# Which instruction carries a semaphore wait: a relation-aware graph attention layer, every repeated wait moved onto the instruction behind it

## The reference

```python
Q = (jnp.einsum('nc,rch->rnh', x, Wq) + bq[:, None, :]).reshape(R, N, HEADS, OUT)
K = (jnp.einsum('nc,rch->rnh', x, Wk) + bk[:, None, :]).reshape(R, N, HEADS, OUT)
V = (jnp.einsum('nc,rch->rnh', x, Wv) + bv[:, None, :]).reshape(R, N, HEADS, OUT)
q_i = Q[edge_type, dst]
k_j = K[edge_type, src]
v_j = V[edge_type, src]
score = jnp.sum(q_i * k_j, axis=-1) * scale
seg = dst * R + edge_type
m = jax.ops.segment_max(score, seg, num_segments=N * R)
e = jnp.exp(score - m[seg])
s = jax.ops.segment_sum(e, seg, num_segments=N * R)
alpha = e / s[seg]
out = jax.ops.segment_sum(v_j * alpha[..., None], dst, num_segments=N)
x = _layernorm(x + out.reshape(N, HD) + bias)
```

## Time and profile before

| | |
|---|---|
| median of 3 runs | 2276.77 us (2274.12 to 2283.94) |
| the profiled execution: its time / span of its instructions | 2263.78 us / 2262.0 us |
| instruction records | 33,259 |
| PE busy | 1719.4 us, 76% of the span |
| DVE busy | 1569.7 us, 69% |
| POOL busy | 1176.7 us, 52% |
| ACT busy | 1074.7 us, 48% |
| DMA | 571.56 MB, mean 253 GB/s |
| chain that ended last | PE 53%, DVE 18%, "issue" 16% |

### The profile page before, as it was taken

One profiled execution on the slowest core, in us unless ns is written; L12 is line 12 of the kernel. 1 busy time (PEld: TensorE's weight loads), 2 busy tenths in 40 slices (PEclk: granted clock), 3 DMA queues, 4 the chain that ended last, 5 costly groups with the idle time before them and its releaser, 6 DMA issues.

```text
span 2262.0 us, 33259 instructions
## 1 busy us (share of the span) xinstructions
PE 1719.4 (76%) x7549; PEld 1186.0 (52%) x7549; DVE 1569.7 (69%) x3858; ACT 1074.7 (48%) x4050; POOL 1176.7 (52%) x1254
## 2 busy tenths in 40 slices
PE   8999995227999995477777777777777777677788
PEld 4555542002444442356666566665666666566667
DVE  8888983002434442587788888887888888888877
ACT  3333320001000000066777777777777777777775
POOL 3111117773666304556666666666666666666504
PEclk9999997657999997699899999999999999999998
DMA  8998737775999747888888889888888998888733
GB/s 225 275 246 226 217 119 231 229 222 185 313 338 329 260 159 234 265 275 265 268 279 282 281 283 283 279 288 281 277 281 286 279 285 284 276 272 278 235 99 114
DMA packets 344898, 571.56 MB, mean 253 GB/s; under 512 B 44993, under 2 KB 238433, under 8 KB 344702
## 3 DMA queue, kind: packets, MB, share of 16 engines
q0 software_dynamic: 87360, 274.23, 40.8%
q1 hardware_dynamic: 224330, 234.48, 31.7%
q10 hardware_dynamic: 33012, 60.73, 7.5%
HBM read 408.84 MB, written 140.96 MB: 243 GB/s over the span
## 4 chain that ended last, share of the span: by engine, by line
PE 53%; DVE 18%; issue 16%; another core or an unknown queue 8%; ACT 3%; POOL 1%; DVEq 1%; DMA 1%; SPq 0%; ACTq 0%; POOLq 0%
PE sums L727 20%; PE sums L796 15%; PE pairs L807 12%; DVE region L1122 3%; DVE region L1323 3%; DVE region L1380 2%; PE bank L762 2%; PE bank L755 1%; DVE region L1332 1%; PE sums L854 1%; POOL region L555 1%; PE sums L865 1%; DVE region L1333 1%; DVE region L1389 1%
## 5 line engine op out<-in xcount | busy, mean ns | idle before, releaser
L555 POOL DMA_INDIRECT region<-kv_tab,kvidx x824 | 806.0, 978 | 566.5 <-issue 198.2
L727 PE MATMUL sums<-region,acc 128*128 128x512 f32 (+2 forms) x1568 | 677.8, 584 | 6.5 <-ACT acc L879 4.1
L994 ACT ACTIVATE region<-region 128x64 f32<-128x64 f32 x2368 | 655.5, 346 | 0.9
L796 PE MATMUL sums<-region 128*128 128x150 f32 x3296 | 500.4, 306 | 129.9 <-issue 125.1
L807 PE MATMUL pairs<-region 128*128 128x256 f32 x1648 | 426.1, 403 | 186.1 <-DVE region L1323 103.4
L796 PEld LDWEIGHTS sums<-region 128*128 128x128 f32 x3296 | 461.4, 199 | 188.6 <-issue 175.6
L727 PEld LDWEIGHTS sums<-region,acc 128*128 128x128 f32 (+1 forms) x1568 | 297.6, 195 | 306.7 <-issue 286.7
L807 PEld LDWEIGHTS pairs<-region 128*128 128x128 f32 x1648 | 312.5, 199 | 249.6 <-issue 210.1
L1291 DVE TENSOR_TENSOR region<-sums,region 128x512 f32<-128x512 f32 (+1 forms) x215 | 147.4, 691 | 368.2 <-PE sums L727 146.2
L1012 ACT COPY acc<-sums 128x294 f32 x824 | 327.2, 397 | 73.5 <-PE sums L796 47.4
L537 POOL DMA_INDIRECT region<-q_tab,region x288 | 274.8, 954 | 147.7 <-issue 81.0
(11 more groups left out here) (244 smaller groups left out, 967.6 us busy)
## 6 DMA issues: line engine op xcount, KB each, us to landing
region<-q_seg SPq DMA_DIRECT2D x824, 128.0 KB
kv_tab<-region ACTq DMA_DIRECT2D x42, 1280.0 KB
q_seg<-region SPq DMA_DIRECT2D x288, 128.0 KB
q_tab<-region SPq DMA_DIRECT2D x48, 640.0 KB, 4.3
region<-rel_tab SPq DMA_DIRECT2D x206, 128.0 KB
region<-region POOLq DMA_DIRECT2D x47, 384.0 KB, 5.5
region<-kv_tab,kvidx POOLq DMA_INDIRECT x824
region<-in_x SPq DMA_DIRECT2D x96, 128.0 KB, 2.8
```

The lines of the kernel that those rows point to most:

```text
L555: pool.indirect_dma_start(ring_row[:, a:a + 2 * C], None, kv_tab, bass.IndirectOffsetOnAxis(ap=kvidx[:, t:t + 1], axis=0)).then_inc(s_got[ ...
L727: done = nc.tensor.matmul(bank[o % 4][0:n, 0:w], acc[:, k, t * P:t * P + n], w_sb[:, k, :, :].rearrange("p u c -> p (u c)")[:, c0:c0 + w], ...
L796: done = nc.tensor.matmul(bank[i][:, h * W:(h + 1) * W], ring_v[:, i, spot(q), h * P:(h + 1) * P], oneh[:, q % 2, i, :], start=True, stop= ...
L994: done = nc.scalar.activation(ring_v[:, i, spot(q), h * D:(h + 1) * D], ring_v[:, i, spot(q), h * D:(h + 1) * D], ACT.Copy, scale=alT[:, h ...
```

## The change

It moves waits from `wait_ge` in front of an instruction onto the instruction itself (`wait_op`), always the last of the waits in front. No wait is dropped and no work moves. The core of the diff:

```diff
@@ -368,11 +368,12 @@
+        def evicted(o):
+
+            return (s_evA, o + 1) if o < OA else (s_evD, o - OA + 1)
+
         def wait_evicted(eng, o):
-            if o < OA:
-                eng.wait_ge(s_evA, o + 1)
-            else:
-                eng.wait_ge(s_evD, o - OA + 1)
+            eng.wait_ge(*evicted(o))
@@ -544,17 +545,17 @@
                     pool.wait_ge(s_agg, SB * (s - KS + KL + 1))
-                if s >= KL:
-
-                    pool.wait_ge(s_mul, s - KL + 1)
...
-                    pool.indirect_dma_start(ring_row[:, a:a + 2 * C], None, kv_tab,
-                                            bass.IndirectOffsetOnAxis(ap=kvidx[:, t:t + 1], axis=0)
-                                            ).then_inc(s_got[s % KL], 16)
+                    rows_in = pool.indirect_dma_start(ring_row[:, a:a + 2 * C], None, kv_tab,
+                                                      bass.IndirectOffsetOnAxis(ap=kvidx[:, t:t + 1], axis=0)
+                                                      ).then_inc(s_got[s % KL], 16)
+                    if i == 0 and s >= KL:
+
+                        rows_in.wait_op(s_mul, s - KL + 1, "sem-ge")
@@ -721,12 +723,12 @@
-                if o >= 4:
-                    wait_evicted(pe, o - 4)
                 for k in range(KC):
...
+                    if k == 0 and o >= 4:
+                        done.wait_op(*evicted(o - 4), "sem-ge")
@@ -785,9 +787,6 @@
-                    if q > 0:
-
-                        pe.wait_ge(s_cols, columns_taken(q - 1, i))
...
+                        if h == 0 and q > 0:
+
+                            done.wait_op(s_cols, columns_taken(q - 1, i), "sem-ge")
                     done.then_inc(s_agg, 1)
 
             def lift(s):
 
                 pe.wait_ge(s_gotq[s % QS], 16 * SB * (s // QS + 1))
                 pe.wait_ge(s_oht, s + 1)
-                if s > 0:
-                    pe.wait_ge(s_mul, s)
                 for i in range(SB):
                     done = nc.tensor.matmul(qk[:, i, :], oht[:, s % 2, i * P:(i + 1) * P], qring[:, s % QS, i, :],
                                             start=True, stop=True)
+                    if i == 0 and s > 0:
+                        done.wait_op(s_mul, s, "sem-ge")
@@ -1006,11 +1007,11 @@
             def place_window(q, i, at):
                 t = q * SB + i
-                act.wait_ge(s_agg, t + 1)
                 if t > 0:
                     act.wait_ge(s_placed, t)
                 nc.scalar.copy(acc[:, :, bass.ds(at[(q % 2) * SB + i] + 1, PW)],
-                               bank[i][:, 0:2 * W].rearrange("p (h n) -> p h n", h=2)[:, :, 0:PW]).then_inc(s_placed, 1)
+                               bank[i][:, 0:2 * W].rearrange("p (h n) -> p h n", h=2)[:, :, 0:PW]
+                               ).then_inc(s_placed, 1).wait_op(s_agg, t + 1, "sem-ge")
@@ -1308,25 +1309,24 @@
                 dve.wait_ge(s_got[s % KL], gathered(s))
-                dve.wait_ge(s_lift, s + 1)
                 if s > 0:
                     dve.wait_ge(s_sc, s)
-                nc.vector.tensor_tensor(prod[:], ring_k[:, :, spot(s), :], qk[:], ALU.mult).then_inc(s_mul, 1)
+                nc.vector.tensor_tensor(prod[:], ring_k[:, :, spot(s), :], qk[:], ALU.mult
+                                        ).then_inc(s_mul, 1).wait_op(s_lift, s + 1, "sem-ge")
@@ -1406,10 +1406,10 @@
                 if i == 0 or q >= SINGLE:
                     dve.wait_ge(s_cols, columns_taken(q, i))
+                added = nc.vector.tensor_tensor(acc[:, :, bass.ds(col, 1)], acc[:, :, bass.ds(col, 1)],
+                                                cols[:, q % CS, i, :, 2:3], ALU.add).then_inc(s_acc, 1)
                 if t > 0:
-                    dve.wait_ge(s_acc, t)
-                nc.vector.tensor_tensor(acc[:, :, bass.ds(col, 1)], acc[:, :, bass.ds(col, 1)],
-                                        cols[:, q % CS, i, :, 2:3], ALU.add).then_inc(s_acc, 1)
+                    added.wait_op(s_acc, t, "sem-ge")
```

## The result

The changed kernel took 2371.44 us, median of 4 executions (2365.69 to 2380.02), the kernel before 2277.84 us. The ratio is 1.041, 95% interval 1.039 to 1.043. Forecast was 2273 us, range 2253 to 2287. In a later comparison, on chip 3, it was 2340.59 against 2264.76 us, ratio 1.034 (1.031 to 1.037).

What follows compares the result with a forecast made beforehand. The loop was taken to run at the pace of POOL's gather bursts with their gap. Savings of 1.1 and 2.8 us less POOL's 0.7 made 3.2, rounded to 3.5: 2276.8 - 3.5 = 2273 us, range 2253 to 2287.

Steps and rivals of the forecast that it cites:

- the POOL exchange: Loop gathers: s_agg moves to the separate wait, losing at most 0.06 us where truly late, 0.7 us in all.
- The 12: Loop: number of steps whose gather comes just behind its aggregate, 0.27 us later, and so truly waits for it.
- The 0.06 us: Loop gathers on POOL: most that each truly late wait loses by standing in the separate instruction, priced as on PE.
- Rival B: Loop, each step's first gather: late s_agg in the separate wait costs 0.06 us, 11.3 us over 188 steps; 2285; chance 0.10.
- The other parts: Loop and its end: ACT and PE give back 1.1 us in 12 steps, the last 14 steps 2.8 us.
- rival C: Loop: a 0.1 us shift moves single steps between prompt and late news of PE's work; 2267 or 2287; chance 0.13.
- rival A: Loop: hand-offs, not POOL, set the pace; 0.20 us less in each of 206 steps, 41 us, 2236, or 2263; chance 0.22.
- The 0.09 us of the sum: Loop on ACT: saved per place_window copy whose aggregate ends last; 0.063 us from wait and arithmetic, more from earlier issue.
- The second stage: From 560 to 880 us: PE is full, so exchanged waits of evictions and chunks give 0; query gathers are not waited for.
- `lift` comes sooner: Loop on PE: lift starts 0.05 us behind products instead of 0.11, saving 0.06 us that matters only if DVE is held.
- The tail: Last 14 steps, without POOL gathers: one waited place and two back to back save 0.20 us a step, 2.8 us.
- The clock: PE's granted clock, read as 0.97 to 0.99 throughout, the upper of its two levels.

Runs made afterwards that it cites:

- ACT's part alone: Kernel before with only the edit on ACT: the copy of place_window carries s_agg, its arithmetic runs ahead, evictions carry s_proj; ratio 1.0015 (0.9998 to 1.0033).
- PE alone: Kernel before with only the edit on PE: matmuls carry s_cols, s_mul and the evictions; s_oh, s_gotq and the weights stand ahead; ratio 0.9995 (0.9978 to 1.0013).

## Why the prediction was wrong, by its steps

**The step that failed** is the count in the POOL exchange: "12 steps like the earlier trace rows x 0.06 = 0.7 us". Both factors were wrong.

- The 12. I took a gather for truly late only where it starts 0.27 us behind the drawn end of the aggregate. But the time at which a wait can pass is that of the update's arrival, and it lies 1.47 us behind that end in the median. Measured from the arrival, the gather's distance is 0.259 us in 175 of 180 steps. I had the right observation in hand, news of PE's work that comes 1.1 us behind the burst, and used it to explain ACT and DVE; I did not ask what it made of the same wait on POOL. That "the gap of 1.27 to 1.29 us before the first gather has the same length where the aggregate is long done" was read as POOL's own pace, from two gaps of one cycle. Over the loop that gap varies from 0.92 to 1.41 us; it was the late news plus 0.259 us.
- The 0.06 us. It came from PE. On POOL the same exchange costs 0.739 - 0.259 = 0.48 us, eight times as much. The trace of before had no row for it, since no gather there stood behind a separate wait that came last.

**Rival B** named the place, the queue and the order of the two waits, and even its condition (POOL's burst is the pace, so every step pays). Its price made it 11 us: 188 x 0.06. With 0.48 it is 90 us, and the whole change measured 94 us (2371.44 - 2277.84). Its chance of 0.10 rested on the same count of 12. The range ended at 2287 us, just above B's 2285, because the unknown cost on POOL was bounded with a row of another engine. The gap of POOL between two gathers without any wait, 0.31 us, was a nearer row than PE's 0.05; it would have made B 188 x 0.31 = 58 us.

**A second term was off.** The other parts were to give 4 us. With the loop gathers undone they cost 24 us (1.009), and the mechanism is open. It looks like rival C: the steps with a gather within 0.3 us of its aggregate's drawn end, 11 in 180 before, are 23 there. The sum of rival A has a slip beside it, 0.05 us for the aggregate where its part says 0.06, which changes nothing.

**The 0.09 us of the sum**, for a copy of `place_window` that is waited for, was met. Of the 824 copies 82 start 0.105 to 0.113 us behind the last update of `s_agg` before, most often 0.109; with ACT's part alone one does, and 104 start 0.019 to 0.026 us behind it, most often 0.023. That is 0.086 us less, where the two records that stood ahead give 0.063; what makes the rest, no run shows. The arithmetic ends 0.041 us ahead of such a copy before and 1.10 us ahead of it in the changed kernel (medians). All the same ACT's part alone measured 1.0015.

**What held.** The stages ahead of the loop are unchanged. The second stage, too, for the reason given. `lift` comes sooner:

```profile
1108.12 1.18 DVE L1322 TENSOR_TENSOR region<-region,pairs 128x1024 f32<-128x1024 f32 x1
...
1109.36 0.30 PEld L807 LDWEIGHTS pairs<-region 128*128 128x128 f32 x2 [0.92 <-issue]
```

1109.36 - 1109.30 = 0.06 us against 0.11 in the earlier trace rows, and is worth nothing (PE alone 0.9995), as said: what is saved ends in a later wait. The tail, forecast 2.8 us shorter: from the last `products` to the end 116.5 us before, 113.6 with ACT's part alone and 113.8 in the second profile of the changed kernel, but 117.4 in its first; profiles without the edit's ACT part have 114.8 to 117.8. Single profiles do not settle 3 us. Rival A (12 to 41 us faster) is out, and so is C as the cause of the loss: on chip 3 it comes with the one exchange alone and goes, but for 0.9%, when this is undone.

**The clock.** The trace of before records the granted clock as 1.00 or 0.50 and nothing between, 80 records in all; a mean is a share of the two. It was not 0.97 to 0.99 throughout, as the prediction has it: from 365 to 560 us it was 0.64. In the changed kernel PE's granted clock fell from 0.97 to 0.90 in the loop, and PE's busy time per step rose from 4.50 to 912.3 / 186.25 = 4.90 us. With the exchange on POOL alone, in which PE's own stream is that of before, it falls the same way, from a mean of 0.930 over the span to 0.897. So it follows from the exchange and its longer step. What the lower clock itself costs was not measured.

**Behind the 0.48 us.** That the gather must still be fetched when the separate wait is through, as rival B and theory G1 have it, was my estimate. What is measured is 0.259 us from the update to a gather that carries the late wait and 0.739 us to one behind it; no run shows what POOL does in between. The record of a separate wait does not tell it either: before the change, where that wait had passed, its record stands 0.037 us behind the update of `s_agg`. So the reason for the 0.48 us stays open; that it is paid is measured.

## What to carry to other kernels

Of several waits in front of one of POOL's indirect gathers, the one that comes last belongs on the gather, and the ones that have long passed belong ahead of it; then those ahead are free (0.259 us from update to gather with a passed wait ahead and with none). The wrong order cost 0.48 us each time it was met, eight times the 0.06 us read on PE, and nothing on chip 12 (0.9988), where neither wait was met late. An exchange of waits on one engine is priced with a row of that engine, or left with a wide bound. And lateness is read from the arrival of the semaphore's update, not from the end of the instruction that sends it: a constant distance from update to start in all steps is the sign of a wait that binds.

## What the hardware showed that was not expected

- The same program takes 1919 us on one chip and 2263 to 2265 us on three others. On these, PE's semaphore updates arrive late while POOL issues indirect gathers: 1.38 us in the median of the loop, 15.4 us at the turn in the earlier trace rows, against 0.014 us. Those of DVE and ACT, where recorded, do not (0.010 and 0.008 us), and in the loop many updates of all engines have no record.
- A rest of POOL at every fourth query gather restores them there (median 0.015 us from 365 to 560 us, PE busy 192 of 195 us), not in the loop behind it, which has no such rest (1.32 us); at every eighth or sixth it does not (3.4 and 6.3 us). What in the chip keeps them back, and why only on some chips, stays open.
- In the kernel before, the record of the separate wait for `s_mul`, a semaphore that had been reached some 13 us earlier, stands 0.037 us behind the update of `s_agg` that the next instruction carried. The start of such a record is no time at which its own semaphore came.
